# Splitting two DMA-transpose stages by rows, and moving the weight loads and a short tail, in an eight-core attention and FFN kernel

## The reference, cut to what matters

```python
def attn(x, Wq, Wk, Wv):                    # x (4, 4096, 1024), W (1024, 64)
    q, k, v = x @ Wq, x @ Wk, x @ Wv
    att = softmax(einsum('bid,bkd->bik', q, k), axis=1)   # over the queries i
    return tile(att @ v, (1, 1, 16))
def ffn(x, W_r, W_k, W_v, mu_r, mu_k):      # W (1024, 1024)
    x_prev = x shifted by one token, zero ahead of the first
    xr = mu_r * x + (1 - mu_r) * x_prev
    xk = mu_k * x + (1 - mu_k) * x_prev
    return sigmoid(xr @ W_r.T) * (square(relu(xk @ W_k.T)) @ W_v.T)
x = x + attn(layernorm(x), ...)
x = x + ffn(layernorm(x), ...)
```

## Time and profile before

| | |
|---|---|
| median of 3 runs | 795.39 us (794.45 to 796.48) |
| the profiled execution's own time | 796.09 us |
| its span (core 7, the slowest) | 794.1 us |
| spans of the 8 cores | 774.5 to 794.1 us |
| busy share of the span | PE 45%, DVE 34%, ACT 33%, POOL 6% |

### The profile page before, as it was taken

The page is one execution under the profiler, slowest core; times in us unless marked ns, Lnnn a source line. Parts: engine busy times, 40 slices in busy tenths (PEclk is TensorE's granted clock), DMA queues, the critical chain, the costliest instruction groups (busy, mean ns, idle before and its releaser), DMA issues.

```text
span 794.1 us, 5653 instructions; the slowest of 8 cores (774.5 to 794.1 us)
## 1 busy us (share of the span) xinstructions
PE 356.1 (45%) x1392; PEld 124.1 (16%) x1392; DVE 273.7 (34%) x499; ACT 262.8 (33%) x452; POOL 47.6 (6%) x77
## 2 busy tenths in 40 slices
PE   0000000000399588888776100000022799999996
PEld 0000000000143011111111100000000343444432
DVE  3321556510075011111113254440599000222666
ACT  2220223300000788888884184410000323332000
POOL 3101111210000000000000211000000000001110
PEclk9999999999999555555665555555556899999999
DMA  9996664569600100000000567749300000002886
GB/s 239 188 191 139 219 230 159 192 169 202 125 1 7 27 7 7 7 0 1 0 1 0 105 230 263 305 170 161 64 0 0 1 0 1 1 0 65 304 261 218
DMA packets 79133, 84.60 MB, mean 107 GB/s; under 512 B 59421, under 2 KB 59437, under 8 KB 79038
## 3 DMA queue, kind: packets, MB, share of 16 engines
q1 hardware_dynamic: 65598, 51.92, 23.4%
q0 software_dynamic: 13504, 32.32, 16.1%
HBM read 47.79 MB, written 30.15 MB: 98 GB/s over the span
## 4 chain that ended last, share of the span: by engine, by line
DMA 32%; PE 23%; DVE 15%; issue 12%; SPq 9%; ACT 8%; DVEq 1%; ACTq 0%; POOL 0%; POOLq 0%
DMA xst<-x_in 11%; PE ktp L876 7%; PE rps L834 6%; DMA zdram<-zst 6%; ACT p_sb L552 6%; DMA v_sb<-vdram 5%; SPq L378 5%; DMA y_out<-x2b 4%; DMA x1dram<-x1b 3%; SPq L771 3%; DVE xr L804 2%; DVE xk L813 2%; PE dpool L492 2%; PE qk L396 2%; PE qk L401 2%
## 5 line engine op out<-in xcount | busy, mean ns | idle before, releaser
L552 ACT ACTIVATE p_sb<-dpool,negm 128x1024 bf16<-128x1024 f32 x128 | 140.8, 1126 | 22.5 <-DVE negm L517 20.7
L834 PE MATMUL rps<-wrT,xr 128*128 128x512 bf16 x256 | 59.2, 396 | 170.1 <-DVE xr L804 150.5
L492 PE MATMUL dpool<-qrep,krep 64*128 64x512 bf16 x256 | 106.1, 586 | 38.2 <-ACT p_sb L552 32.7
L396 PE MATMUL qk<-zT,wqk 128*128 128x512 bf16 x64 | 16.8, 410 | 211.1 <-DMA zT<-zdram 211.1
L363 DVE TENSOR_REDUCE sums<-xst 128x1 f32<-128x1024 f32 x32 | 39.0, 1220 | 58.9 <-DMA xst<-x_in 58.9
L934 PE MATMUL ops<-wvT,kaT 128*128 128x512 bf16 x256 | 56.4, 379 | 5.2 <-DVE tmp L980 3.5
L834 PEld LDWEIGHTS rps<-wrT,xr 128*128 128x128 bf16 x256 | 25.8, 101 | 203.1 <-issue 175.5
L876 PE MATMUL ktp<-xk,wkT 128*128 128x512 bf16 x256 | 55.6, 379 | 1.7 <-ACT r_sb L847 1.3
L523 DVE TENSOR_REDUCE ell<-ellp 128x1 f32<-128x4 f32 x32 | 5.0, 157 | 135.0 <-ACT p_sb L552 135.0
L901 DVE TENSOR_TENSOR kaT<-krl 128x512 bf16<-128x512 bf16 x32 | 13.6, 425 | 97.5 <-ACT krl L892 97.4
L396 PEld LDWEIGHTS qk<-zT,wqk 128*128 128x128 bf16 x64 | 6.5, 103 | 219.3 <-issue 212.7
(11 more groups left out here) (83 smaller groups left out, 394.7 us busy)
## 6 DMA issues: line engine op xcount, KB each, us to landing
xst<-x_in SPq DMA_DIRECT2D x32, 512.0 KB, 8.4
zdram<-zst POOLq DMA_DIRECT2D x32, 256.0 KB, 8.0
xst<-x_in POOLq DMA_DIRECT2D x16, 512.0 KB, 12.5
x1dram<-x1b SPq DMA_DIRECT2D x16, 512.0 KB, 4.3
xst<-x1dram POOLq DMA_DIRECT2D x16, 512.0 KB, 6.2
y_out<-x2b SPq DMA_DIRECT2D x16, 512.0 KB, 4.5
z1dram<-z1b SPq DMA_DIRECT2D x16, 256.0 KB, 3.6
wrT<-wrT_in POOLq DMA_DIRECT2D x1, 2048.0 KB, 43.8
```

Source lines behind the costliest of these rows:

```text
L396: t.matmul(qk[buf][:, :], wqk[:, ct * 128:(ct + 1) * 128], zT[ct][:, nch * 512:(nch + 1) * 512], start=(ct == 0), stop=(ct == CT - 1), ski ...
L492: t.matmul(units[u][:, cc * 512:(cc + 1) * 512], krep[64 * a:64 * (a + 1), kt * 128:(kt + 1) * 128], qrep[64 * a:64 * (a + 1), c * 512:(c ...
L552: sc.activation(p_sb[kt % 4][:, s * 1024:(s + 1) * 1024], units[u][:, :], AF.Exp, bias=negm[:, kt:kt + 1], accum_out=ellp[:, 4 * (kt % 2) + s:
L834: ins = t.matmul(r_ps[t_ % 2][:, hh * 512:(hh + 1) * 512], xr[ct][:, t_ * 128:(t_ + 1) * 128], wrT[:, ct * C + hh * 512:ct * C + (hh + 1) ...
```

## The change

It has four parts. The three large weight loads are issued by POOL after all `zdram` stores instead of ahead of them. The first transpose is cut into four quarters of 1024 rows, eight DMA transposes each, issued by ACT after the sqrt of every second group, once the stores of that group have landed; PE waits for one quarter at a time. In the second layer norm the sum moves from ACT's Copy to a DVE `reduce_sum`, and the tail (extra row and zero blocks) moves ahead of the loop on DVE, ACT and SP. The second transpose is issued by ACT in two halves of 1088 rows: the first half's eight together, then the second half's eight, each waiting for the one before to land; DVE waits for them one column tile at a time.

```diff
             g.dma_start(out=ident[:, :], in_=ident_in).then_inc(SW, 16)
-            g.dma_start(out=wrT[:, :].rearrange("p (ct d) -> p ct d", d=C),
-                        in_=wrT_in.rearrange("(ct p) d -> p ct d", p=128)).then_inc(SWB, 16)
...
                             in_=zst[:, s * C:(s + 1) * C]).then_inc(ZAs[s], 16)
+            g.dma_start(out=wrT[:, :].rearrange("p (ct d) -> p ct d", d=C),
+                        in_=wrT_in.rearrange("(ct p) d -> p ct d", p=128)).then_inc(SWB, 16)
...
                 sc.activation(sstd[:, gb:gb + 4], svar[:, gb:gb + 4], AF.Sqrt,
                               bias=cconst[:, 0:1]).then_inc(SS, 1)
+                if g % 2 == 1:
+                    qtr = (g - 1) // 2
+                    for s in range(4):
+                        sc.wait_ge(ZAs[s], 16 * (2 * qtr + 2))
+                    for ctn in range(CT):
+                        sc.dma_start(out=zT[ctn][:, qtr * 1024:(qtr + 1) * 1024],
+                                     in_=zdram[qtr * 1024:(qtr + 1) * 1024,
+                                               ctn * 128:(ctn + 1) * 128],
+                                     transpose=True).then_inc(SZQ[qtr], 16)
...
-        @block.sync
-        def _(sy):
-            for s in range(4):
-                sy.wait_ge(ZAs[s], a_za(TT - 4 + s))
-            for ctn in range(CT):
-                sy.dma_start(out=zT[ctn][:, :],
-                             in_=zdram[:, ctn * 128:(ctn + 1) * 128],
-                             transpose=True).then_inc(SZT, 16)
...
-            t.wait_ge(SZT, SZT_B)
             for nch in range(8):
+                t.wait_ge(SZQ[nch // 2], 128)
...
# SP, second layer norm: row 63 and the two zero blocks now ahead of the stores
+            sy.wait_ge(SV, SV_F0 + 10)
+            sy.dma_start(out=z1dram[63:64, :], in_=z1xm).then_inc(SD, 16)
...
# DVE, second layer norm
+                v.wait_ge(SV, F_CNT[("x1", t_)])
+                if t_ >= 8:
+                    v.wait_ge(SV, F_CNT[("smean", (t_ - 8) // 4)])
+                v.reduce_sum(sums[:, s8:s8 + 1], x1b[:, s8 * C:(s8 + 1) * C],
+                             axis=AX.X).then_inc(SV, 1)
...
+            v.wait_ge(SD, sd_xlast)
+            v.tensor_tensor(x1x, xlast, ...)      # the whole tail, ahead of the loop
...
# ACT, second layer norm: the tail's Square and Sqrt first, and in the loop
-                    sc.activation(junk[:, :], x1b[:, (t_ % 8) * C:(t_ % 8 + 1) * C],
-                                  AF.Copy,
-                                  accum_out=sums[:, t_ % 8:t_ % 8 + 1]).then_inc(SS, 1)
...
+        @block.scalar
+        def _(sc):
+            sc.wait_ge(SD, sd_zero1)
             for s in range(4):
-                sy.wait_ge(ZSs[s], zs_f(12 + s))
+                sc.wait_ge(ZSs[s], zs_f(4 + s))
             for ctn in range(CT):
-                sy.dma_start(out=z1T[ctn][:, :],
+                sc.dma_start(out=z1T[ctn][:, 0:1088],
+                             in_=z1dram[0:1088, ctn * 128:(ctn + 1) * 128],
+                             transpose=True).then_inc(SG_LO, 16)
+            sc.wait_ge(SD, sd_zero2)
+            for s in range(4):
+                sc.wait_ge(ZSs[s], zs_f(12 + s))
+            sc.wait_ge(SG_LO, 128)
+            for ctn in range(CT):
+                sc.wait_ge(SG_HI, 16 * ctn)
+                sc.dma_start(out=z1T[ctn][:, 1088:2176],
+                             in_=z1dram[1088:2176, ctn * 128:(ctn + 1) * 128],
+                             transpose=True).then_inc(SG_HI, 16)
...
             for ct in range(CT):
+                v.wait_ge(SG_HI, szt_g_hi(ct))
```

More of the change, by code:

```diff
@@ L132, in build_program @@
         ZAs = [e(nc.semaphore(f"ZA{i}")) for i in range(8)]
-        SZT = e(nc.semaphore("SZT"))
+        SZQ = [e(nc.semaphore(f"SZQ{i}")) for i in range(4)]
+        SG_LO = e(nc.semaphore("SG_LO"))
+        SG_HI = e(nc.semaphore("SG_HI"))
         SM = e(nc.semaphore("SM"))
@@ L155, in plan_ln @@
                         cnt[(op, i)] = sv
-                    if include_sum:
-                        sv += 1
-                        cnt[("sum", i)] = sv
+                    sv += 1
+                    cnt[("sum", i)] = sv
                 if g >= 1:
@@ L294, in _ @@
                             in_=zst[:, s * C:(s + 1) * C]).then_inc(ZAs[s], 16)
+            g.dma_start(out=wrT[:, :].rearrange("p (ct d) -> p ct d", d=C),
+                        in_=wrT_in.rearrange("(ct p) d -> p ct d", p=128)).then_inc(SWB, 16)
+            g.dma_start(out=wkT[:, :].rearrange("p (ct d) -> p ct d", d=C),
+                        in_=wkT_in.rearrange("(ct p) d -> p ct d", p=128)).then_inc(SWB, 16)
+            g.dma_start(out=wvT[:, :].rearrange("p (ct d) -> p ct d", d=C),
+                        in_=wvT_in.rearrange("(ct p) d -> p ct d", p=128)).then_inc(SWB, 16)
         @block.scalar
@@ L648, in _ @@
         def _(sy):
+            sy.wait_ge(SV, SV_F0 + 10)
+            sy.wait_ge(SD, sd_row63 - 16)
+            sy.dma_start(out=z1dram[63:64, :], in_=z1xm).then_inc(SD, 16)
+            sy.wait_ge(SV, SV_F0 + 11)
+            sy.wait_ge(SD, sd_zero1 - 16)
+            sy.dma_start(out=z1dram[0:63, :],
+                         in_=bass.AP(zst, 0, [[4 * C, 63], [1, C]])).then_inc(SD, 16)
+            sy.wait_ge(SD, sd_zero2 - 16)
+            sy.dma_start(out=z1dram[2112:2176, :],
+                         in_=bass.AP(zst, 0, [[4 * C, 64], [1, C]])).then_inc(SD, 16)
             for g in range(4):
@@ L684, in f_apply_emit @@
                                     ALU.mult, ALU.add).then_inc(SV, 1)
+            v.wait_ge(SD, sd_xlast)
+            v.tensor_tensor(x1x, xlast,
+                            bass.AP(outx_row, 0, [[D, 1], [0, 16], [1, D]]),
+                            ALU.add).then_inc(SV, 1)
+            v.wait_ge(SV, SV_F0 + 1)
+            v.reduce_sum(rs[:, 0:1], x1x, axis=AX.X).then_inc(SV, 1)
+            v.wait_ge(SS, SS_F0 + 1)
+            v.wait_ge(SV, SV_F0 + 2)
+            v.tensor_scalar(rs[:, 2:3], rs[:, 0:1], cconst[0:1, 2:3], None, ALU.mult).then_inc(SV, 1)
+            v.tensor_scalar(rs[:, 3:4], rs[:, 1:2], cconst[0:1, 2:3], None, ALU.mult).then_inc(SV, 1)
+            v.wait_ge(SV, SV_F0 + 3)
+            v.tensor_tensor(rs[:, 4:5], rs[:, 2:3], rs[:, 2:3], ALU.mult).then_inc(SV, 1)
+            v.wait_ge(SV, SV_F0 + 5)
+            v.tensor_tensor(rs[:, 5:6], rs[:, 3:4], rs[:, 4:5], ALU.subtract).then_inc(SV, 1)
+            v.wait_ge(SS, SS_TAIL)
+            v.reciprocal(rs[:, 7:8], rs[:, 6:7]).then_inc(SV, 1)
+            v.wait_ge(SV, SV_F0 + 7)
+            v.scalar_tensor_tensor(rs[:, 8:9], rs[:, 2:3], cconst[0:1, 1:2], rs[:, 7:8],
+                                   ALU.mult, ALU.mult).then_inc(SV, 1)
+            v.wait_ge(SV, SV_F0 + 8)
+            v.tensor_scalar(z1x, x1x, rs[:, 7:8], rs[:, 8:9],
+                            ALU.mult, ALU.add).then_inc(SV, 1)
+            v.wait_ge(SW, SW_SMALL)
+            v.wait_ge(SV, SV_F0 + 9)
+            v.tensor_scalar(z1xm, z1x, hmask[0:1, 0:1], None,
+                            ALU.mult).then_inc(SV, 1)
+            v.memset(zst[:, 0:C], 0.0).then_inc(SV, 1)
             for g in range(4):
@@ L694, in _ @@
             f_apply_emit(v, 3)
[L695 to L721, removed]
         @block.scalar
         def _(sc):
+            sc.wait_ge(SV, SV_F0 + 1)
+            sc.activation(jrow, x1x, AF.Square,
+                          accum_out=rs[:, 1:2]).then_inc(SS, 1)
+            sc.wait_ge(SV, SV_F0 + 6)
+            sc.activation(rs[:, 6:7], rs[:, 5:6], AF.Sqrt, bias=cconst[0:1, 0:1]).then_inc(SS, 1)
             for g in range(4):
```

54 lines of the change are left out of this document (12 added, 42 removed).

## The result

The changed kernel is slower. Its median is 811.48 us (809.82 to 817.73, 10 runs) against 796.03 (794.45 to 829.82, 10 runs) for the kernel before; the ratio is 1.020, 95% interval 1.0175 to 1.0224. The forecast was 776, range 754 to 803. Rival (b), the starving last quarter, named the place of the larger miss, and gave 802. Of the runs of the kernel before, the one at 829.82 was in a slower state of the chip and is not in the ratio.

What follows compares the result with a forecast made beforehand. Both layer norms and their transposes hold PE idle, so v's store and the end of `xr` count: 17.5 + 1.5 = 19 us less than the profiled 796.1 makes 777, as a median 776; range 754 to 803.

Steps and rivals of the forecast that it cites:

- Rival (b): First layer norm: last quarter's transposes starve until the weights land; v's store 8 us late, 802 us; chance 0.18.
- Weights' removal from the front: First layer norm: without the weights ahead, group 0 applied at 21 and group 1 at 37.5; worth about 36 us.
- ACT's stall: First layer norm: ACT waits for stores, then issues eight transposes (15.6 us); a quarter takes 50.9 us against 33.
- Rival (a): ACT's transpose issues cost 1.1 us each; each of three quarters shrinks by 6.8 us; 756 us; chance 0.17.
- The last quarter beside the weights: End of first layer norm: last quarter's transposes take 27 us beside the weight loads, ends 17 and 44, landing at 214.3.
- "weights first" end: Upper end for the last quarter's transposes: about 44 us if the weight loads came first.
- the equal share: Last quarter: transposes share the DMA engines equally with the weight loads and need about 22 us; 27 taken.
- Projections: After the first layer norm: two chunks and v remain, 24.8 us from the last landing to v's store at 239.1.
- The tail at the front: Second layer norm: the tail ahead of the loop makes the loop start 14.3 us late.
- The loop: Second layer norm: groups 22 us apart; first x1 to the end of the last apply +3.0 us.
- The second transpose: After second layer norm: first half lands about 556, second half 3.7 us a piece; `xr` ends 1.5 us earlier.
- rival (c): Second transpose: one-by-one second half costs 5 us a piece, 10 us lost in the second part; 787 us; chance 0.15.

Runs made afterwards that it cites:

- w_after_q: The changed kernel, but POOL issues the three large weight loads only when the last quarter's transposes have landed; 780.24 us, ratio 0.980 to the kernel before.
- sp_first: The kernel before with first-transpose quarters issued from SP, x loads from the ninth on from POOL, weights behind v's transposes; 739.46 us, ratio 0.922.

## Why the prediction was wrong, by its own steps

- **Weights' removal from the front: right, 4.6 us short.** Group 1 applied at 42.1 on core 2, forecast 37.5. I had group 0 at 21 where it came at 24.9: the eighth x tile was hardly earlier without the large weights.
- **ACT's stall: right in size, in part by luck, since errors cancel.** Quarter 50.3 and 48.9 for 50.9. Eight issues took 12.6 us, not 15.6: an issue of 1024 rows alone costs 1.3 us, where the line through 64, 2176 and 4096 rows gave 1.95. Rival (a) had this, at 1.1; its reason, back-pressure of the longer transposes, is not shown. The wait for the stores took 13.6 instead of 11.5, and the release to the next apply 7.7 instead of 7.3.
- **The last quarter beside the weights: the step that failed.** I took 27 us between ends of 17 and 44. It was 50.4 (185.36 to 235.7 on core 2; 49.0 to 51.1 over the cores), beyond my upper end: 23 us of the 35 between forecast and result. Two terms failed. The first is the share: I took it near equal, and the packets show one of the transposes for one of the loads, 0.61 MB against 4.92 in 33 us, so the quarter lands last. The second is the price of the loads: I had 33 us for the three, from the spacing of two landings, and `w_after_q` shows 42 to 44 with little beside them. With 43 my "weights first" end would have been 54 from their issue, 51 from the first transpose's. I chose near the equal share for want of a row of a transpose beside other traffic. The row of a 256-byte DMA between x loads, 5.8 us from its issue to the next, was in my own evidence and spoke for rival (b): the tail's 2 KB row, behind all stores in the kernel before, is done within 1.3 us (528.95 to 530.23, L756). I used the 5.8 for the tail alone.
- **Projections: right.** 24.4 us from the last landing to v's store (235.72 to 260.14), forecast 24.8. Only two chunks were left.
- **The tail at the front: mechanism right, size short.** First x1 18.1 us later, forecast 14.3: from the issue of the second small DMA to that of the third it was 5.4 to 6.0 us on cores 0, 3, 5 and 7, and 11.2 to 13.4 on cores 1, 2, 4 and 6; I took 5.8 from one core. The kernel before has 11.6 and 12.7 there on cores 0 and 3, so the trace that I had could have told.
- **The loop: short.** +6.6, forecast +3.0. Groups were 22.1 and 21.6 apart on core 2, as forecast (22); of the rest, the last group's apply came 6.6 us after the one before it instead of 4.6, and its last tile waited 4.6 us for a z1 store, a wait that I had not in the sum.
- **The second transpose: right on the second half, wrong on the first.** The second half went at 3.5 us a piece (3.7 forecast); rival (c)'s 5 never came. The first half took 29 us to its landing on core 2, not 19.5. That the stage still took 49.7 us on the mean, forecast 48.7, is luck in part: the first half began 8.4 us ahead of the end of the last apply instead of 3.7, and the second half was 2 us shorter.

So rival (b) held, with a lower price than I gave it in the first part (5.9 us late instead of 8) and none of my 1.5 us of gain in the second, where 9.2 were lost. My chances were also added up wrong: by the list, faster comes to 0.82 and not 0.78.

## What to carry to other kernels

Before a transfer is moved off one queue's path, look at what it will stand beside where it goes: a DMA transpose beside plain traffic in large rows crawls (18 GB/s here, against some 184 alone) until that traffic is done, and so a load that is "hidden" behind it is paid in full; a wait that keeps the two apart cost nothing where the loads came behind v's transposes too (`sp_first`, attention 183.7 us), and 5 us where v's store stood beside them (`w_after_q`). Issue transposes from an engine that nobody waits for. And a chain of tiny DMAs at the start of a load burst is slow (5 to 13 us for each of the three here), so leave it behind other work unless something waits for it.

## What the runs showed of the hardware that was not expected

A transpose of 1024 rows x 128 columns is issued in 1.3 us alone and in up to 15.6 us beside weight loads; eight of them take 12 us more for each 4 MB read beside them, cast or not, from POOL or from SP. Beside the weight loads the engines pass as many packets of one queue as of the other, 2433 and 2433 in 33 us, though one kind has eight times the bytes. The Trainium skill (page "Advanced Engine Details and Errata", section on the X-bar transpose) gives 350 to 400 GB/s for transposes: 2.1 MB in the 11.6 us of issue are 181 GB/s, near the 192 of the whole transpose in the kernel before, so the measurement disagrees here too, with all eight cores at it.

TensorE's granted clock fell from 1.0 to 0.50 (the 1.2 GHz level) after the first early `qk` chunks in the layer norm, when PE stood idle again, where the kernel before held 1.0 until attention; the mean fell from 0.79 to 0.70. It cost nothing that the stage table shows, since the stages of attention and of the end took what they took before, within 2 us.
